# Six one-hots side by side: a wider stride for TensorE and fewer instructions for VectorE in a graph network's block builder

## The reference

```
edge_index = jnp.stack([src, dst])
h = jnp.maximum(_layernorm(x, axis=-1), 0.0)
x = x + _L0_gnn_ref(h, ..., src, dst, edge_type_200)     # softmax weights a, sum of a * h[src] into dst
x = x + _L1_gnn_ref(h, edge_index, ...)                  # counts of edges
x = x + _L2_gnn_ref(h, edge_weight, src, dst)            # sums with edge_weight, twice
x = x + _L3_gnn_ref(h, edge_index, ...)                  # eight heads, 64 -> 8*64
```

## Time and profile before

| | |
|---|---|
| Median of 3 runs | 4098.42 us (4097.68 to 4103.26) |
| The profiled execution's own time | 4094.57 us |
| Its span, first to last instruction | 4092.8 us |
| TensorE matmul busy | 2133.9 us (52%) |
| TensorE weight load busy | 1646.5 us (40%) |
| VectorE busy | 2004.1 us (49%) |
| ScalarE busy | 550.9 us (13%) |
| GpSimd busy | 1035.2 us (25%) |

### The profile page before, as it was taken

How to read it: one execution, slowest core, us unless ns; L and a number is a source line. 1 busy time by engine, 2 the same in 40 slices (tenths; PEclk the granted TensorE clock), 3 DMA queues, 4 the chain that set the end, 5 groups by cost and what they waited for, 6 DMA issues and landing times.

```text
span 4092.8 us, 45162 instructions
## 1 busy us (share of the span) xinstructions
PE 2133.9 (52%) x14866; PEld 1646.5 (40%) x14917; DVE 2004.1 (49%) x3088; ACT 550.9 (13%) x1109; POOL 1035.2 (25%) x984
## 2 busy tenths in 40 slices
PE   1448628888869989930000677730111000777684
PEld 1312227777769933320000566630010000666653
DVE  5899868777750031020000799997000000555584
ACT  0000014444423410000000222211100000000000
POOL 0040050000000000047776000047777775000000
PEclk9558768888869989965555899975555555999975
DMA  1143223233334557722121000003332111022030
GB/s 57 4 128 121 68 41 131 125 137 137 133 141 160 190 211 269 293 55 52 46 69 45 0 0 0 0 13 134 121 90 51 30 33 40 24 76 76 7 71 8
DMA packets 130791, 346.36 MB, mean 85 GB/s; under 512 B 52088, under 2 KB 54051, under 8 KB 122629
## 3 DMA queue, kind: packets, MB, share of 16 engines
q1 hardware_dynamic: 62101, 169.08, 11.8%
q10 hardware_dynamic: 36560, 141.07, 9.6%
q0 software_dynamic: 32032, 34.94, 4.7%
HBM read 219.96 MB, written 124.90 MB: 84 GB/s over the span
## 4 chain that ended last, share of the span: by engine, by line
PE 35%; DVE 23%; another core or an unknown queue 18%; issue 15%; DVEq 2%; ACT 1%; DMA 1%; POOL 0%; ACTq 0%; POOLq 0%
PE PS L1198 7%; PE PS L1278 4%; PE PS L1162 3%; DVE big L1798 3%; PE PS L1233 3%; PE PS L1122 2%; PE PS L1099 2%; DVE big L1918 2%; PE PS L1170 2%; PE PS L1096 2%; DVE big L1970 2%; PE PS L1277 2%; PE PS L1223 2%; DVE s_ring L1647 1%
## 5 line engine op out<-in xcount | busy, mean ns | idle before, releaser
L666 POOL DMA_INDIRECT ring<-d_h,idx_lin x784 | 814.0, 1038 | 1274.1 <-DMA d_h<-Hn 550.1
L1278 PE MATMUL PS<-arena,s_ring 128*128 x1968 | 299.2, 274 | 281.8 <-issue 223.7
L1918 DVE TENSOR_TENSOR big<-PS,qa 128x800 f32<-128x800 f32 x196 | 192.8, 984 | 437.1 <-remote 254.1
L1970 DVE TENSOR_TENSOR big<-big,PS 128x512 f32 x123 | 84.6, 687 | 643.1 <-remote 371.4
L1223 PE MATMUL PS<-big 128*125 128x128 bf16 x784 | 133.4, 296 | 454.7 <-issue 304.6
L1278 PEld LDWEIGHTS PS<-arena,s_ring 128*128 128x128 f32 x1968 | 307.3, 205 | 117.1 <-issue 97.3
L1096 PE MATMUL PS<-big,qa 128*128 128x225 bf16 x1050 | 292.7, 292 | 115.2 <-DVE big L1798 113.7
L1099 PE MATMUL PS<-big,qa 128*128 128x150 bf16 x2100 | 310.7, 254 | 0.0
L1223 PEld LDWEIGHTS PS<-big 128*125 128x125 bf16 x784 | 106.6, 209 | 500.7 <-issue 308.4
L1233 PE MATMUL PS<-big,arena 125*128 125x200 bf16 x2352 | 252.9, 261 | 102.6 <-ACT arena L893 68.3
L1798 DVE TENSOR_TENSOR big<-big,qa 128x900 bf16<-128x900 bf16 x525 | 296.6, 621 | 0.0
(11 more groups left out here) (444 smaller groups left out, 3696.2 us busy)
## 6 DMA issues: line engine op xcount, KB each, us to landing
big<-d_blk SPq DMA_DIRECT2D x24, 2000.0 KB, 7.7
d_blk<-big ACTq DMA_DIRECT2D x13, 3125.0 KB, 9.0
big<-d_blk SPq DMA_DIRECT2D x25, 1562.5 KB, 6.4
d_blk<-arena ACTq DMA_DIRECT2D x12, 3125.0 KB, 9.0
big<-d_blk SPq DMA_DIRECT2D x12, 2250.0 KB, 8.1
d_stash<-ring SPq DMA_DIRECT2D x98, 256.0 KB
arena<-d_stash ACTq DMA_DIRECT2D x98, 256.0 KB
ring<-d_h,idx_lin POOLq DMA_INDIRECT x784
```

Of the source, the lines that this page charges most:

```text
L666: pool.indirect_dma_start(ring[:, HALF * h + s, :], None, table, bass.IndirectOffsetOnAxis(ap=idx_lin[:, CH * i + s:CH * i + s + 1], axis= ...
L1278: mm = nc.tensor.matmul(PS[:, bass.ds(place[s] + j % SUMS * BANK, D)], marks[:, j % 2, s, :], arena[:, bass.ds(at[s], D)], start=False, st ...
L1918: v_.tensor_tensor(picked.rearrange("p (s h k) -> p s h k", s=CB, h=H), free(PS[:, 0:1], [[BANK // 2, CB], [NB, H], [1, NB]], 2 * j * BANK ...
L1970: v_.tensor_tensor(acc[:, bass.ds(base, BANK)], acc[:, bass.ds(base, BANK)], bank(j % SUMS, P, BANK), ALU.add).then_inc(S["step_added"], 1)
```

## The change

All six steps of a part lie side by side for each key: key 0 of steps 0 to 5, key 1 of steps 0 to 5, and so on. The innermost run is six elements in place of two. The weighted groups of all six steps are one instruction of 2700 elements per partition in place of three of 900. TensorE reads a step at a stride of six elements, 12 bytes, in place of two, 4 bytes, both for the weights that it loads (`step_lo`) and for the columns that it streams (`step_c`). The values and the number of TensorE's instructions are the same; the buffers keep their sizes and places.

```diff
-        def pairs_lo(h):
-            return free(hots_lo[:, 0:1], [[2 * W, QP], [2, W], [1, 2]], h * HOT_LO)
-        def pairs_c(h):
-            return free(hots_c[:, 0:1], [[14 * CW, QP], [2, CW], [1, 2]], h * HOT_C)
-        def pair_c(h, p, first, n, step):
-            return free(hots_c[:, 0:1], [[step * 2 * CW, n], [2, CW], [1, 2]], h * HOT_C + p * 14 * CW + first * 2 * CW)
+        def hot_row(t, at, n):
+            return free(t[:, 0:1], [[QB, n], [1, QB]], at)
+        def part_c(h, first, n, step):
+            return free(hots_c[:, 0:1], [[step * QB * CW, n], [QB, CW], [1, QB]], h * HOT_C + first * QB * CW)
         def step_lo(h, s):
-            return free(hots_lo[:, 0:1], [[2, W]], h * HOT_LO + s // 2 * 2 * W + s % 2)
+            return free(hots_lo[:, 0:1], [[QB, W]], h * HOT_LO + s)
         def step_c(h, s, first, n):
-            return free(hots_c[:, 0:1], [[2, n * CW]], h * HOT_C + s // 2 * 14 * CW + first * 2 * CW + s % 2)
+            return free(hots_c[:, 0:1], [[QB, n * CW]], h * HOT_C + first * QB * CW + s)
...
-            lo_iota, c_iota = (free(iota_q[:, 0:1], [[0, QP], [2, n], [1, 2]]) for n in (W, CW))
-            pair_lo, pair_key = (free(key_tab[:, 0:1], [[2, DP // 2], [0, n], [1, 2]], q * DP) for q, n in ((0, W), (1, CW)))
+            lo_iota, c_iota = (free(iota_q[:, 0:1], [[2, n], [0, QP], [1, 2]]) for n in (W, CW))
             at_lo, at_c = (free(key_tab[:, 0:1], [[0, n], [1, DP]], q * DP) for q, n in ((0, W), (1, CW)))
...
-                half, k, k2 = c % 2, of_part(i, c, QB), of_part(i, c, QP)
+                half, k = c % 2, of_part(i, c, QB)
                 v.wait_ge(S["part_done"], of_part(i, c) + 1)
-                v_.tensor_tensor(pairs_c(half), c_iota, pair_key[:, bass.ds(k2, QP), :, :], ALU.is_equal).then_inc(S["hot_ready"], 1)
-                v_.tensor_tensor(pairs_lo(half), lo_iota, pair_lo[:, bass.ds(k2, QP), :, :], ALU.is_equal)
+                v_.tensor_tensor(hot_row(hots_c, half * HOT_C, CW), c_iota, at_c[:, :, bass.ds(k, QB)], ALU.is_equal).then_inc(S["hot_ready"], 1)
+                v_.tensor_tensor(hot_row(hots_lo, half * HOT_LO, W), lo_iota, at_lo[:, :, bass.ds(k, QB)], ALU.is_equal)
                 v.wait_ge(S["hot_ready"], of_part(i, c) + 1)
-                for p in range(QP):
-                    last = v_.tensor_tensor(pair_c(half, p, 1, 6, 1), pair_c(half, p, 0, 6, 0), at_wa[:, :, :, bass.ds(k + 2 * p, 2)], ALU.mult)
+                last = v_.tensor_tensor(part_c(half, 1, 6, 1), part_c(half, 0, 6, 0), at_wa[:, :, :, bass.ds(k, QB)], ALU.mult)
                 last.then_inc(S["one_ready"], 1)
```

## The result

The changed kernel takes 4604.1 us (median of 6 runs) against 4098.3 before: a ratio of 1.1234, 95% interval 1.1218 to 1.1249, so 506 us or 12% slower. One of the six was a slow run of 4875 us, which the ratio leaves out. The forecast was slower, 4158, with a range up to 4215. The direction held, the size missed by a factor of eight (506 against 60 us).

The account below looks back on a forecast made before the run. TensorE was taken to pace about 17 us of each block, VectorE 6 to 7. 2.6 us more in each of 24 blocks, 61, less 1.3 in the first, gave +60: 4158 against 4098.4, range 4089 to 4215.

Parts of the forecast that it names:

- VectorE's side: One multiplication for three per part: 1.47 us in place of 1.61 to the next hots, at most 8 us in all.
- the rival's remark that the clock may take it back: No-cost case: blocks may meet the long lower-clock stretch more often, eating up the 0.28 us a block; 4090 to 4098.
- the bound on TensorE's side: Range for a TensorE step at 12 bytes: from 0.24 us, no cost, to 0.44, one column in two cycles.
- nothing at the lower clock, where a column has twice the time: Steps at the lower clock lose nothing to the 12-byte stride; those at the higher lose 0.10 us each.
- the forecast's 0.34: Step at the higher clock, halfway between 0.24 and 0.44 us, next to three weight loads of 0.109; 0.30 to 0.38 had 45%.
- the eight steps at the lower clock: Of 36 steps in each block's TensorE-bound stretch, eight run at the lower clock; the other 28 lose 2.8 us.
- 1.5 times a step (0.35 us): Estimate by the skill's page: four elements at 12 bytes touch three 16-byte lines, step 0.35 us, about +66 us.
- full-cost rival: TensorE's step at the higher clock takes 0.44 us, one column in two cycles: +144 us, 4242; chance 12%.
- VectorE's pace: Rival: VectorE's multiplication falls from two elements a cycle to one, 2.9 us, +128 us; chance 2%.
- no cost: Rival: TensorE's stride costs nothing, step stays 0.24 us, VectorE's 8 us are gained or lost to the clock; 33%.
- The small cost in the weight loads: Rival: only TensorE's weight loads slow, mostly hidden behind the columns: +5 to +40 us; chance 8%.
- Slower by more than 0.2%: Forecast outcome for the whole kernel: slower by more than 0.2%, 8 us, about what a measurement can tell; chance 65%.

Follow-up runs that it names:

- e5: Kernel before with weights laid out pair by pair, so one multiplication of 2700 elements does a part; 4-byte stride kept: 3279.5 against 3281.2 us.
- e6: Changed kernel with both of TensorE's operands read at the 4-byte stride and addresses of the kernel before (wrong products): 3279.1 against 3281.2 us.
- e12: e11 with the single multiplication of e5, against the kernel before: 3207.3 against 3278.6 us, ratio 0.9778.
- e11: Kernel before with 16 matmuls of zeros behind each overflow, in TensorE's gap before part 2: 3211.7 against 3278.6 us, ratio 0.9793.
- e1: Kernel before with only TensorE's loaded weights at a stride of 12 bytes (wrong products): 4104.4 against 4093.4 us.
- e10: Kernel before with TensorE's streamed columns at a stride of 2 bytes (wrong elements): 3276.0 against 3278.6 us.
- e7: Kernel before with steps 3 to 5 of each part streamed at 12 bytes, steps 0 to 2 at 4 (wrong elements): 3528.5 against 3281.2 us.
- e8: Kernel before with streamed columns at a stride of 16 bytes, from the table of weights (wrong elements): 4020.8 against 3281.2 us.
- e9: Kernel before with streamed columns at a stride of 32 bytes, from the table of weights (wrong elements): 4039.2 against 3278.6 us.
- e3: Kernel before with streamed columns at a stride of 8 bytes (wrong elements): 4260.0 against 4093.4 us.
- e4: Kernel before with streamed columns at a stride of 6 bytes (wrong elements): 4179.1 against 4093.4 us.
- e2: Kernel before with only the streamed columns at a stride of 12 bytes, weights at 4 (wrong products): 4593.8 against 4093.4 us.

## Why the prediction was wrong

**VectorE's side** held in each number: 1.56 us for the multiplication, 1.48 us from its start to the next hots (929.79 to 931.27, forecast 1.47), comparisons at 0.40 and 0.55, the wait before part 1 gone, the one before part 2 at 3.71. The most that it could give was put at 8 us, and the rival's remark that the clock may take it back fits e5 and e6 (medians 2 us from the kernel before, inside the interval; the pattern of stretches in e6), with e12 against e11 as the case in which it doesn't, as far as one trace of each shows.

**The step that failed** is the bound on TensorE's side: "The high end is the step at the lower clock, 0.44, which is one column for two cycles." It measured 0.70 at the higher clock and 0.71 at the lower. Nothing in the row of the lower clock limits what a read can cost; it was a row about another cause, taken as the end of a range because it was the slowest step at hand. With it fell "nothing at the lower clock, where a column has twice the time": 12 bytes need 1.33 ns a column, and two cycles last 0.83. In the sum's own terms a step at the higher clock loses 0.46 us and not 0.10, and one at the lower 0.27 and not nothing. The nearest rows at 8 and 12 bytes were weight loads, and three loads of 0.109 us were what the forecast's 0.34 leaned on. e1 shows that they spoke of another reader: a load at 12 bytes takes 125 ns, beside the matmuls, and moves a step by 7 ns. So the right direction came with a reason that doesn't hold, and was in part luck. That left 2 and 4 bytes as the only evidence on streaming, and the two sit at the knee, where most of the cost is hidden behind a column a cycle; that they cost the same was not quite so either (e10: 17 ns a step).

**What followed from it** and was not in the sum: the clock. The forecast kept the eight steps at the lower clock of each block; in fact all of the stage ran at 0.50. There five aggregation products take 1.98 us rather than 1.05 (e7). Put together, a block is 42 steps x 0.713 = 29.9 us, 5 aggregations x 1.98 = 9.9, the gap 3.7 and some 0.6 for the overflow, 44.1; its starts are 44.2 apart. Against aggregation at the higher clock throughout, that is 5 x 0.93 = 4.6 us a block. The kernel before had lost part of this already: in its trace the loop's blocks have on average 12.6 us of steps and 6.8 of aggregation, in the changed kernel's 29.9 and 9.9. So of the 506 us the steps are some 415 (24 x 17.3) and the aggregation some 75 (24 x 3.1); the first block has much of the rest. Most of the miss is thus the price of a step, and the clock comes second. This split is worked out and no run had 12 bytes at the higher clock throughout.

**The Trainium skill's rule.** SBUF — State Buffer, Specifications, of the Trainium skill had the right unit: the 16-byte line shows in e8 and e9, where the cost stops growing. As forecast from it, 1.5 times a step (0.35 us), it misses: two hits on a line (8 bytes, e3) do not give full bandwidth but about half of it, 0.91 ns a column at the higher clock against 0.47. The later remark on the same page of the Trainium skill (Door 1: The DMA port swizzle) that one can stride 8 bfloat16 for free is refuted for this operand by e8: 0.933 us a step at 1.2 GHz, where 4 bytes take 0.441.

**The chances.** Slower by more than 0.2% had 65%, which came. The size lay beyond even the full-cost rival (4242), so no case of the forecast named it; that rival only added that it would be more if the steps at the lower clock slowed too, as they did. The two rivals of VectorE's pace and of no cost are out by the timelines: the multiplication is 1.56 and not 2.9 us, the step not 0.24. The small cost in the weight loads, mostly hidden, is there (e1), but under the large one.

**What stays open.** Why the clock stays at 0.50 although TensorE is shown busy for 1006 of 1105 us; e8 and e9 never leave it either, e3 and e4 are at it for 10.2 us in most blocks, and e7 for 458 of 838 us. Why the load is lengthened so much less than the streaming, and what it would cost behind shorter matmuls, wasn't tried.

## What to carry to other kernels

Give the operand that TensorE streams a stride of at most 4 bytes (bfloat16 in pairs), and leave a wider one (12 bytes were tried, behind matmuls of 150 columns and more) to the loaded operand. When a term has no row of its own, the slowest row at hand is no upper bound: ask whether it is slow for the same reason. And before saving tenths of a microsecond in a block with a gap on TensorE, look at what the clock does after the gap; filling it with zeros gave 67 us, while the saving gave some 5, and that only once the gap was filled.

## What the runs showed of the hardware

- Streaming costs 1.77 ns for each 16 bytes passed over, up to one such piece a column, or a TensorE cycle a column where that is longer: 0.93 us for 525 columns at 16 bytes, 0.95 at 32, and 0.70 to 0.71 at 12 at either clock (e2, e7, e8, e9). Loading 128 columns at 12 bytes takes 125 ns in place of 98, of which a step here feels 7 (0.253 against 0.246 us, e1).
- With all steps streamed at 12 bytes or more the stage stays at a granted clock of 0.50 (1092 us of it; also e2, e8, e9), and the aggregation products are slowed with it, 1.98 against 1.05 us. With 6 or 8 bytes, or half the steps at 12 (e3, e4, e7), it doesn't.
- A smaller gap on TensorE can go with more time at the lower clock: in e6 218 us of it against 181, and a saving of 0.28 us a block doesn't reach the time. With the gap filled the granted clock is 0.99, and a block takes 20.85 us in place of 24.02 (e11).
- The kernel before takes 4098 us on one chip and 3281 on another. This stage is as long on both (594 us, and 591 to 594 in e5, e6 and e10); why the others differ stays open.
